# Gathering the embedding rows in five overlapping chunks of 106 instead of four of 128

## The reference: what is computed

```
e = stack([tbl_f[ids[:, f]] for f in range(39)], axis=1)      # 512 x 39 x 32
z = einsum('bpc,apc,bpa->bp', e[:, ROW, :], w, e[:, COL, :])  # 741 pairs
h = concatenate([z, dense_ctx], axis=1)                       # 512 x 757
h = maximum(h @ W_top1 + b_top1, 0)                           # 512 x 512
h = maximum(h @ W_top2 + b_top2, 0)                           # 512 x 256
y = h @ W_top3                                                # 512 x 1
```

## Time and profile before

| what | value |
|---|---|
| time, median of 2 runs | 291.04 us (289.72 and 292.36) |
| span of the profiled execution | 285.0 us |
| PE busy | 198.8 us (70%) |
| DVE busy | 146.6 us (51%) |
| POOL busy | 134.8 us (47%) |
| ACT busy | 97.5 us (34%) |
| indirect transfers | 108, of 971 ns of POOL each on average |

### The profile page before, as it was taken

One profiled execution on the slowest core, in us unless ns is written; L12 is line 12 of the kernel. 1 busy time (PEld: TensorE's weight loads), 2 busy tenths in 40 slices (PEclk: granted clock), 3 DMA queues, 4 the chain that ended last, 5 costly groups with the idle time before them and its releaser, 6 DMA issues.

```text
span 285.0 us, 2687 instructions
## 1 busy us (share of the span) xinstructions
PE 198.8 (70%) x974; PEld 73.5 (26%) x974; DVE 146.6 (51%) x115; ACT 97.5 (34%) x142; POOL 134.8 (47%) x134
## 2 busy tenths in 40 slices
PE   0048668453212277738798197699899999999996
PEld 0012223000000033213333032243333334344341
DVE  0353794101000027824794266389599779898230
ACT  2516899300000047830540071037127127110032
POOL 7774767777777300776587887200042015007000
PEclk9999797755555559795999669599999999999999
DMA  4869779700000003997266018148715846450000
GB/s 134 257 210 300 285 177 212 164 16 13 14 13 13 9 0 74 300 207 148 50 158 166 12 41 183 41 96 167 167 33 118 183 98 129 98 121 1 0 2 0
DMA packets 11352, 31.40 MB, mean 110 GB/s; under 512 B 3230, under 2 KB 7098, under 8 KB 10379
## 3 DMA queue, kind: packets, MB, share of 16 engines
q1 hardware_dynamic: 7882, 29.45, 42.1%
q0 software_dynamic: 3456, 1.78, 3.5%
HBM read 12.34 MB, written 0.00 MB: 43 GB/s over the span
## 4 chain that ended last, share of the span: by engine, by line
PE 51%; issue 18%; DMA 9%; DVE 7%; SPq 6%; another core or an unknown queue 4%; ACT 3%; DVEq 0%; ACTq 0%
PE t_ps L719 16%; PE z_ps L735 15%; PE z_ps L688 9%; DMA mlp<-tbl 6%; PE side_ps L750 5%; DMA wring<-w_lo 4%; DVE prod L658 3%; SPq L425 2%; PE t_ps L777 2%; DVE prod L629 2%; SPq L431 1%; SPq L475 1%; PE t_ps L765 1%; PE t_ps L770 1%
## 5 line engine op out<-in xcount | busy, mean ns | idle before, releaser
L658 DVE TENSOR_TENSOR prod<-t_ps,eT 128x1536 f32<-128x1536 f32 (+2 forms) x70 | 109.9, 1600 | 79.3 <-PE t_ps L719 49.7
L514 POOL DMA_INDIRECT gathered<-tbl,ids_sb x108 | 104.9, 971 | 53.5 <-issue 31.4
L719 PE MATMUL t_ps<-stack,wring 128*128 128x512 f32 x210 | 72.9, 464 | 12.2 <-issue 6.7
L735 PE MATMUL z_ps<-prod,sel 128*32 128x512 f32 x380 | 57.5, 645 | 4.6 <-issue 4.6
L719 PEld LDWEIGHTS t_ps<-stack,wring 128*128 128x128 f32 x210 | 38.3, 205 | 65.8 <-issue 39.5
L688 PE MATMUL z_ps<-prod,room 125*32 125x512 bf16 x72 | 21.0, 534 | 34.1 <-issue 33.3
L528 POOL TENSOR_TENSOR room<-room,w_hi 128x512 f32<-128x512 f32 x3 | 3.9, 1286 | 66.3 <-ACT w_hi L603 66.3
L629 DVE TENSOR_SCALAR prod<-mlp,slice_rows 125x2048 bf16<-125x2048 f16 x18 | 14.8, 856 | 23.0 <-remote 23.0
L587 ACT ACTIVATE stack<-hi_lo 32x512 fp32r<-32x512 f32 x39 | 24.6, 629 | 2.6 <-issue 1.2
L580 ACT ACTIVATE stack<-eT 32x512 fp32r<-32x512 f32 x39 | 24.4, 625 | 1.0 <-PE t_ps L719 0.7
L750 PE MATMUL side_ps<-room,mlp 128*128 128x512 f32 x32 | 18.4, 660 | 7.7 <-ACT eT L567 7.6
(11 more groups left out here) (49 smaller groups left out, 113.5 us busy)
## 6 DMA issues: line engine op xcount, KB each, us to landing
wring<-w_hi SPq DMA_DIRECT2D x30, 224.0 KB
wring<-w_lo SPq DMA_DIRECT2D x30, 224.0 KB
stack<-stack SPq DMA_DIRECT2D x9, 512.0 KB
w_lo<-wst SPq DMA_DIRECT2D x4, 896.0 KB, 15.2
eT<-hot_ids SPq DMA_DIRECT2D x3, 1024.0 KB
gathered<-tbl,ids_sb POOLq DMA_INDIRECT x108
mlp<-w SPq DMA_DIRECT2D x1, 1536.0 KB
mlp<-tbl SPq DMA_DIRECT2D x12, 125.0 KB
```

What stands on the lines that cost most here:

```text
L514: pool.indirect_dma_start(gathered[:, n % GATHER_BUFS, b, K * r:K * r + K], None, tables[f], bass.IndirectOffsetOnAxis(ap=ids_sb[:, F * b ...
L658: dve.tensor_tensor(prod[:, g % XSLOTS, 0:n, :], t_ps[g % 2][:, 0:n, :], field, ALU.mult).then_inc(multiplied, 1)
L719: mm = pe.matmul(t_ps[g % 2][:, i, :], wring[:, c % WSLOTS, passes % WCHUNK, :].bitcast(F32R), stack[:, J % STACKS, src - G * J, :].bitcas ...
L735: mm = pe.matmul(z_ps[K * (u % G):K * (u % G) + K, :], sel[:, u // G, :], prod[:, g % XSLOTS, t - TILE_BASE[g], :], start=(u < G), stop=(u ...
```

## The change

The number of chunks goes from four to five, and a chunk has 106 rows instead of 128. The chunks start at samples 0, 106, 212, 318 and 406, so samples 406 to 423 are fetched and transposed twice, to the same columns. The ids are laid out on the host to match, 106 partitions of 195 numbers instead of 128 of 156.

```diff
-NCHUNK = B // P
+ROWS = 106
+STARTS = [0, 106, 212, 318, 406]
+NCHUNK = len(STARTS)
...
-            sp.dma_start(ids_sb[:, :], ids).then_inc(ids_in, 16)
+            sp.dma_start(ids_sb[0:ROWS, :], ids).then_inc(ids_in, 16)
...
                     for b in range(NCHUNK):
                         pool.indirect_dma_start(
-                            gathered[:, n % GATHER_BUFS, b, K * r:K * r + K], None, tables[f],
-                            bass.IndirectOffsetOnAxis(ap=ids_sb[:, F * b + f:F * b + f + 1], axis=0),
+                            gathered[0:ROWS, n % GATHER_BUFS, b, K * r:K * r + K], None, tables[f],
+                            bass.IndirectOffsetOnAxis(ap=ids_sb[0:ROWS, F * b + f:F * b + f + 1], axis=0),
                         ).then_inc(rows_in[J], 16)
...
                     for b in range(NCHUNK):
-                        mm = pe.transpose(side_ps[0:n, P * b:P * b + P], gathered[:, at, b, 0:n], ident[:, :])
+                        mm = pe.transpose(side_ps[0:n, STARTS[b]:STARTS[b] + ROWS], gathered[0:ROWS, at, b, 0:n],
+                                          ident[0:ROWS, 0:ROWS])
...
-    arrays["ids"] = np.ascontiguousarray(a["ids"].reshape(NCHUNK, P, F).transpose(1, 0, 2).reshape(P, -1))
+    rows = np.array(STARTS)[None, :] + np.arange(ROWS)[:, None]
+    arrays["ids"] = np.ascontiguousarray(a["ids"][rows].reshape(ROWS, -1))
```

## The result

The changed kernel takes 355.05 us (353.45 and 356.65) against 291.04 us: a ratio of 1.221 with a 95% interval of 1.202 to 1.240. The forecast was 293 us with a range of 278 to 307, so it missed by 62 us. The profiled execution has a span of 351.7 us and took 353.45 us; before, the span was 285.0 us.

The account below looks back on a forecast made before the run. It read the chain of waits as TensorE 51%, "issue" 18%, POOL none. Terms 0 + 0 + 0 + 0.6 + 1.0 = 1.6 us on the 285.0 us span gave 286.6, with 6.0 added 292.6, taken as 293 us; range 278 to 307.

Parts of the forecast that it names:

- Step 1: Each gather on POOL: stays at 1.25 us with its gap, or 1.08; 27 more add 34 or 11 us of POOL.
- faster rival: POOL's gathers become much cheaper, 0.83 us each, and slow stretches shrink with them: 277 to 285 us, chance 0.27.
- Steps 2 to 4: POOL's first stop, blocks 4 to 6 (gathers end at 109.8 us), blocks 7 and 8: idle time covers added gathers, cost 0.
- step 2: POOL's first stop, after block 2's gathers: table rest ends at 30.8 instead of 29.7 us; cost 0, 1 us if late.
- step 4: POOL's blocks 7 and 8: first `w_lo` 2.4 us later, about 149 us, covered by over 40 us; cost 0.
- Step 5: Seven more transposes on TensorE: 0.6 us, between 0.3 and 1.9; five transposes in 0.6 to 0.75 us.
- Step 6: Load of the ids on 106 partitions, ahead of the table loads in SP's queue: 1.0 us, between 0 and 3.
- slower rival: Slow stretches in the third look-up and before 162.4 and 179.9 us last while POOL gathers: 299 to 309 us, chance 0.33.

Follow-up runs that it names:

- experiment 1: The changed kernel with five chunks of 112 rows instead of 106, still 135 gathers: 331.66 us, ratio 1.122 to the kernel before.
- experiment 2: The kernel before with 26 unused gathers of 13 sizes, 128 to 16 rows, behind the real ones: a single run of 313.8 us, against 292.1 beside it.
- experiment 3: The changed kernel with only four chunks of 106 rows fetched, 108 gathers, last samples wrong: 282.44 us, ratio 0.963 to the kernel before.
- experiment 8: The changed kernel with five chunks of 111 rows instead of 106: 305.75 us, ratio 1.072 to the kernel before.
- experiment 4: The kernel before with only the first chunk gathered, 27 gathers instead of 108, other samples wrong: 227.82 us, ratio 0.779.
- experiment 6: The kernel before with a memset of 256 columns behind each gather, 1.44 us from one gather to the next: 251.25 us, ratio 0.879.
- experiment 5: The kernel before with a memset of 704 columns behind each gather, 1.81 us from one gather to the next: 278.37 us, ratio 0.973.
- experiment 9: The kernel before with a memset of 8 columns behind each gather, distance still 1.25 us: 292.50 us, ratio 1.013.
- experiment 10: The kernel before with a memset of 448 columns behind each gather, 1.60 us from one gather to the next: 256.37 us, ratio 0.898.
- experiment 12: The kernel before with a memset of 328 columns behind each gather, 1.50 us from one gather to the next: 243.71 us, ratio 0.842.
- experiment 7: The kernel before with POOL waiting before block 5 until the three look-ups have used their one-hot matrices: 278.14 us, ratio 0.972.

## Why the prediction was wrong

*Step 1, the price of a gather, failed.* I took 0.94 + 0.30 = 1.25 us "since all 108 gathers lie at 0.94 with nothing in the rows that suggests a part by row", with ends of 1.08 and 1.25. It is 1.86, beyond both ends. A constant over rows of one shape says nothing of another shape. Experiments 1, 2, 3 and 8 show the cause: the rows over their largest divisor up to 16, here 53 where it was 8, at 13 ns each. The rule of the Trainium skill that fits this stood in the prediction itself, beside the ids and beside the faster rival, but only with the question which transfers need fewer engines. I read fewer engines as less to pay for, when the price goes with the rows that are left to each. The lower bound of the range took in a cheaper gather and the upper one no dearer one, though the table loads at 70 GB/s against 131 showed the direction.

*Steps 2 to 4, the cover.* Each was worked out as a budget against idle time of POOL, for gathers at 1.25 us. (Even at that distance, in experiment 1, blocks 4 to 6 ended at 114.4 us instead of my 109.8.) At 1.86 us blocks 4 to 6 take 55 x 1.86 = 102 us instead of 69, and the idle 17.68 us is gone. The table rest of step 2, which I gave at most 1 us, ends at 53.8 instead of 29.7, and TensorE waits 24.12 us. TensorE's waits for gathered rows come to 92.2 us. The first `w_lo` is ready at 230.46 + 4.04 = 234.5 us, where step 4 had about 149, and ACT's copy at 249.44 waits 15.69 us for a load of the weight ring from it.

*Step 5, the transposes.* Five take 0.67 us at 58.97, where the granted clock is 1.00 (2.4 GHz), inside the 0.6 to 0.75 I named, and 1.15 us at 104.29, after a wait of 16.90 us, where it is 0.50 (1.2 GHz). The mean is 373 ns; before it was 278. In all the transposes kept TensorE busy for 7.4 us instead of 4.3. These 3.1 us lie above my upper end of 1.9, which took the old record for the seven new ones and left the other 28 as they were. They stand behind waits of 92.2 us, so the slip doesn't matter for the time.

*Step 6, the ids.* The load ended at 4.5 us by the chain's row below, against a first gather at 3.0 us before, so POOL started 1.8 us later (4.83):

```profile
0.80 3.71 DMA ids_sb<-ids
```

The first split of a table came at 9.56 instead of 8.60, the 1.0 that I took. But kernels with ids on 128 partitions had it anywhere from 8.46 to 10.07 (experiments 4 and 6), so that this step came true is not more than luck: the 1 us can't be told from the scatter of the start; the later landing of the ids can.

*The slower rival* had the right mechanism with a price that was too small by half: experiment 1 has its condition, gathers at the old price, and gives 331.66 where it had 309. It took the waits to grow by the length of the added gathers; the look-up alone grew by 21 us for 11 more gathers in blocks 4 to 6, where I had put 8. In the changed kernel it decided nothing, since at a distance of 1.86 us the slow stretch was gone. Two errors of opposite sign stood in the sum: the slow stretch that I left in place gave back about 30 us (copy at 73.74 instead of 103.20), and POOL took that back and 64 us more.

*The faster rival* had the sign of the price wrong. Whether cheaper gathers would have helped wasn't tried; experiments 5, 6, 9, 10 and 12 speak against it, since from 1.50 us down to 1.25 a shorter distance makes the kernel slower.

*Two readings* of mine were off without bearing on the result. In step 2 the idle 2.67 us less 1.25 leave 1.42, which covers the 1.1 us whole. And from 99 us on the third look-up had four matmuls and not five, so the slower rival's 8 us was a little too much by its own rule.

What stays open. Why close gathers go with slow stretches isn't shown: the trace puts those waits down to "issue" and to an unnamed releaser. I speak of TensorE because the look-up creeps there, but experiments 7 and 9 show engines that start late though what they wait for is recorded as done, a memset of POOL among them. That signals between engines arrive late would fit these rows as well as a TensorE that is slow; no experiment tells the two apart. The six gaps, 25.5 us of the changed kernel's span, have no named releaser either; experiments 1 and 8, also with 135 gathers, don't have them, so neither their number nor the five chunks alone make them. And how far the optimum of the distance, here near 1.5 us, depends on this kernel wasn't tried.

## What to carry to other kernels

Choose the rows of an indirect gather so that they have a large divisor up to 16: 112 or 104 rows are cheap, 106 and 127 are not. Then look at the distance as well. By POOL's time five gathers of 112 rows (5 x 1.24 = 6.2 us) are cheaper than four of 106 (4 x 1.86 = 7.4 us), and yet experiment 1 took 331.66 us and experiment 3 took 282.44; only with the pause did the five come out below (277.23). A duration that is constant over one shape bounds nothing for another; where a rule names the resource count, work out the price in both directions. And where TensorE creeps while a queue of small gathers runs beside it, try them a little further apart before making them cheaper: 0.25 us of pause behind each was worth 16% here.

## What the runs showed of the hardware

- A gather of 128-byte rows occupied POOL for about 0.86 us + 0.013 us x r, with r the rows over their largest divisor up to 16, from 0.85 us (16 rows) to 2.54 us (127 rows), and 0.30 us to the next one.
- Behind a memset the gap before a gather was 0.17 us instead of 0.30.
- Beside gathers 1.24 to 1.25 us apart there were slow stretches, in the look-up and in the tiles alike, though not everywhere (68 matmuls in one window of 25 us, 11 in one of 30); 1.43 and 1.44 us left some of them; from 1.50 us on ACT and DVE had no unnamed wait, with 108 gathers or 135.
- In such a stretch transposes recorded as over at 96.69 us were copied by ACT at 130.38, and a memset that waited only for another memset, over for 2 us, sat 0.91 us.
